# Attention's pair in another order on TensorE, VectorE and ScalarE

## The chip, the cores and the metric

One NeuronCore of a Trainium2 chip runs the whole program in one launch. The metric is the device time of one execution in microseconds, from three timed runs.

## The reference, cut to what matters

Four layers work on x, 32 batches of 128 tokens of 144 channels. The first three each hold an attention block and an MLP; the fourth rotates the tokens by a matrix exponential. Only attention is touched:

```python
B, L, C = (8, 128, 144); H = 16; D = C // H          # called with 32 batches
h = _modulate(_layernorm(x), shift_msa, scale_msa)
qkv = h @ W_qkv + b_qkv                              # 144 -> 432
scores = jnp.einsum('blhd,bmhd->bhlm', q * scale, k)
attn = jax.nn.softmax(scores, axis=-1)
o = jnp.einsum('bhlm,bmhd->blhd', attn, v).reshape(b, l, c)
x = x + gate_msa * (o @ W_proj + b_proj)
```

## The kernel before, in words

Each engine runs a list of its own, written out by hand, and waits on semaphores. Attention goes over 16 pairs of batches a layer (`for i in range(NP): pair(i)`); in `pair(i)` the even batch is e = 2i and the odd one o = 2i + 1. The steps of several pairs are interleaved: `at(lag)` tells whether pair i - lag exists, so a call with e - 4 is the even batch of two pairs ago, and one with i + 2 prepares tokens two pairs ahead.

The way of one batch, with the lines of the profile:

- VectorE normalises the tokens (`normalise`, L505 and L508, into xh). TensorE transposes both batches of a pair (`turn`, L1413 and L1414, into PSUM bank 5). ScalarE applies scale and shift (`h_modulate`, four instructions, L1072 and L1074, into hf and hs) and casts the high parts (`h_high`, L1086 and L1087). VectorE makes the low parts (`h_second`, which calls `low_parts`, L511 and L512). This splitting into high and low fp32r parts is the token rounding.
- TensorE multiplies by the QKV weights (`qkv_product`, four matmuls, L1399), into bank 4. ScalarE copies q and k (`qkv_high`, L1099) and V (L1100), and doubles the high parts (`qk_double`, L1107). VectorE writes the low parts of q and k (`qk_low`, L539).
- TensorE transposes q and k (`qk_turned`, four transpositions for each of j = 0 to 3, L1441; j = 0, 1 are the even batch, 2, 3 the odd one; bank 4, for j = 3 bank 5). ScalarE copies them (`qk_copy`, L1114, into Q and KK).
- `scores(b1, b2, a)` (L1456 and L1463) is 16 matmuls: the scores of b1 as rows, for the maximum, into PSA, and those of b2 transposed, for the exponential, into PSB. VectorE takes the row maximum (`row_max`, L544, two of a batch). TensorE transposes it (`max_turn`, L1491), and VectorE adds it into Q (`max_row`, L552). ScalarE takes the exponential of the second scores (`exps`, L1124, two of a batch).
- `pv` (L1480, 16 matmuls, two of a batch) writes bank 6; ScalarE copies it (`out_copy`, L1130); TensorE turns it back (`out_back`, L1501); VectorE divides (`inverse_sums`, L561, `normalise_out`, L566); TensorE transposes again (`out_turn`, L1506 and L1507); ScalarE copies (`oT_copy`, L1136 and L1137); TensorE projects (`project`, L1511 and L1512). VectorE multiplies by the gate (`gated_at`, L516) and adds to x, with new statistics (`update`, L521 and L524).

Waits that matter here: `pv(b, .., 1)` waits for the output copy of the batch before, since there is one bank for PV. `qkv_product(P, 1)` waits for the KK copy of j = 1, which is in the same bank. `scores(b1, b2, a)` waits for the maxima of b1 taken so far, for `max_row(b2)` and for the exponentials of the batch before. `h_modulate(P)` waits for `h_second(P - 1)`. SP loads a gate row for a batch once the update three batches before is done. GpSimd works on a QR factorisation, apart from all this.

The calls before the first pair are `pair(-2)` and `pair(-1)`; `passage` leads from the last pair into the MLP. In some pairs further work is queued: casts and splits of the MLP weights (pairs 2 to 6; in layer 1 these are four times as wide) and the steps of the deviations.

## Time and profile before

| | |
|---|---|
| three timed runs | 1269.46 us median, 1266.23 to 1276.68 |
| profiled execution | 1270.11 us, its span 1267.7 us |
| TensorE, matmuls | 1194.4 us busy, 94% of the span |
| VectorE | 910.0 us, 72% |
| ScalarE | 788.0 us, 62% |
| GpSimd | 749.6 us, 59% |
| chain of work that ended last | TensorE 82%, VectorE 13%, issue 4%, ScalarE 2% |

The share of busy time is an average over stages. Attention's pairs run from about 40 to 235 us (layer 0), 343 to 550 us (layer 1) and 915 to 1115 us (layer 2). Matmuls are pipelined: what a block costs TensorE is read from its start to the start of the next block.

### The profile page before, as it was taken

To read this page: it belongs to the slowest core of one execution; us is meant where nothing else is said; L and a number is where in the kernel's file an instruction comes from. 1 tells how busy PE (TensorE), PEld (TensorE's weight loads), DVE (VectorE), ACT (ScalarE), POOL (GpSimd) and SP (SyncE) were. 2 spreads that over 40 slices of the span, in tenths; PEclk is the share of its full clock that TensorE was granted. 3 is DMA by queue.
4 is the path that set the end of the run, shared out by engine and by line. 5 is a ranking of instruction groups with operands and counts; after the bars stand their busy time and mean duration, and the time that the engine had idled before them with its cause. 6 is when DMAs were issued, how large, how long until landed. Compare 5 with 4: busy or idle time off the path is not lost.

```text
span 1267.7 us, 35439 instructions
## 1 busy us (share of the span) xinstructions
PE 1194.4 (94%) x12778; PEld 949.3 (75%) x12778; DVE 910.0 (72%) x2496; ACT 788.0 (62%) x1809; POOL 749.6 (59%) x2230
## 2 busy tenths in 40 slices
PE   4899999899899999999999999999899999999997
PEld 2677777688676777778888888887777777777775
DVE  6799999766579999965575555554679999955432
ACT  3589898756479898963342333233379888874531
POOL 5656656666656656566676666667777777740000
PEclk9999999999979999999999999999969999989997
DMA  6321121242531121130210111120121111101130
GB/s 171 62 19 19 18 23 16 48 97 33 107 67 20 15 21 16 21 57 5 16 14 5 16 15 7 13 44 20 35 43 27 31 35 33 23 6 20 19 66 28
DMA packets 50319, 42.82 MB, mean 34 GB/s; under 512 B 8455, under 2 KB 45754, under 8 KB 49717
## 3 DMA queue, kind: packets, MB, share of 16 engines
q1 hardware_dynamic: 45884, 29.91, 10.9%
q0 software_dynamic: 3488, 8.52, 8.4%
q8 instruction: 104, 1.70, 0.6%
q10 hardware_dynamic: 780, 2.17, 0.5%
q14 instruction: 63, 0.52, 0.1%
HBM read 33.86 MB, written 3.03 MB: 29 GB/s over the span
## 4 chain that ended last, share of the span: by engine, by line
PE 82%; DVE 13%; issue 4%; ACT 2%; DMA 0%; SPq 0%; ACTq 0%; DVEq 0%
PE PS L1678 18%; PE PSA L1399 15%; PE PSA L1456 8%; PE PS L1480 8%; PE PS L1441 7%; PE PS L1399 6%; DVE BIG L544 3%; PE PSB L1651 2%; PE PS L1511 2%; PE PS L1501 2%; PE PS L1512 2%; PE PSB L1463 1%; PE PS L1506 1%; PE PS L1491 1%; DVE xh L508 1%
## 5 line engine op out<-in xcount | busy, mean ns | idle before, releaser
L1255 ACT ACTIVATE BIG<-PSA 128x512 f32<-128x512 f32 (+1 forms) x224 | 132.0, 593 | 264.1 <-PE PSA L1399 264.0
L1678 PE MATMUL PS<-w,BIG 128*128 128x144 f32 (+1 forms) x1920 | 254.7, 287 | 7.6 <-DVE BIG L818 4.1
L544 DVE TENSOR_REDUCE BIG<-PSA 128x8 f32<-128x1024 f32 x192 | 234.1, 1219 | 31.9 <-PE PSA L1456 29.9
L1678 PEld LDWEIGHTS PS<-w,BIG 128*128 128x128 f32 (+1 forms) x1920 | 245.1, 190 | 15.6 <-DVE BIG L818 4.9
L1124 ACT ACTIVATE BIG<-PSB 128x1024 f32<-128x1024 f32 x192 | 195.5, 1018 | 20.5 <-PE PSB L1463 20.3
L1456 PEld LDWEIGHTS PSA<-KK,Q 32*128 32x128 f32 x1536 | 109.9, 196 | 57.8 <-issue 41.0
L1456 PE MATMUL PSA<-KK,Q 32*128 32x128 f32 x1536 | 135.1, 294 | 14.9 <-DVE BIG L544 4.7
L1441 PE MATMUL PS<-K,qt 128*128 128x128 f32 x768 | 127.3, 293 | 10.4 <-DVE qt L539 4.8
L1463 PE MATMUL PSB<-Q,KK 32*128 32x128 f32 x1536 | 133.9, 293 | 0.0
L1480 PE MATMUL PS<-BIG,VA 128*32 128x128 f32 x3072 | 128.5, 287 | 1.1 <-DVE col L419 1.1
L1893 POOL MEMSET qprod<- 128x2 f32 x63 | 6.2, 99 | 203.0 <-DMA VB<-QA 203.0
L1875 POOL TENSOR_TENSOR qtree<-qtree 128x36 f32<-128x36 f32 (+3 forms) x384 | 104.3, 272 | 30.1
L1441 PEld LDWEIGHTS PS<-K,qt 128*128 128x128 f32 x768 | 91.3, 148 | 34.4 <-DVE qt L539 17.6
L1463 PEld LDWEIGHTS PSB<-Q,KK 32*128 32x128 f32 x1536 | 106.2, 195 | 1.2 <-DVE Q L552 0.4
L1399 PE MATMUL PSA<-hhi,Mhi 128*128 128x512 f32 (+1 forms) x224 | 99.9, 446 | 3.1 <-DVE h L512 2.1
L818 DVE SCALAR_TENSOR_TENSOR BIG<-PS,BIG 128x144 f32<-128x144 f32 x96 | 34.9, 367 | 94.6 <-PE PS L1678 94.0
L1880 POOL TENSOR_TENSOR qtree<-qtree 128x4 f32<-128x4 f32 (+3 forms) x384 | 83.7, 218 | 30.0
L1480 PEld LDWEIGHTS PS<-BIG,VA 128*32 128x32 f32 x3072 | 74.6, 112 | 30.2 <-issue 20.8
L1399 PE MATMUL PSA<-h,MW 128*128 128x512 f32 (+1 forms) x224 | 88.6, 395 | 0.0
L1399 PE MATMUL PSA<-hhi,Mlo 128*128 128x512 f32 (+1 forms) x224 | 88.5, 395 | 0.0
L1399 PE MATMUL PSA<-hlo,Mhi 128*128 128x512 f32 (+1 forms) x224 | 88.1, 393 | 0.0
L1099 ACT ACTIVATE qt<-PS 128x288 fp32r<-128x288 f32 x93 | 41.2, 443 | 56.5 <-PE PS L1399 56.5
(307 smaller groups left out, 2955.8 us busy)
## 6 DMA issues: line engine op xcount, KB each, us to landing
gate<-gates SPq DMA_DIRECT2D x96, 72.0 KB, 2.9
mgate<-gates SPq DMA_DIRECT2D x96, 72.0 KB, 2.7
VB<-skew POOLq DMA_DIRECT2D x16, 288.0 KB, 3.7
X<-in_x SPq DMA_DIRECT2D x4, 576.0 KB, 11.4
out<-X SPq DMA_DIRECT2D x8, 288.0 KB, 3.6
BIG<-in_skew_w SPq DMA_DIRECT2D x2, 1024.0 KB
w<-in_w SPq DMA_DIRECT2D x1, 1440.0 KB, 11.4
BIG<-in_wqkv SPq DMA_DIRECT2D x2, 584.0 KB
```

The costliest lines, as they stand in the source:

```text
L544: V.tensor_reduce(nmax.rearrange("p (s w) -> p s w", w=HP)[:, 2 * a:2 * a + 2, 3 * HD:3 * HD + G], PSA[:, :].rearrange("p (r g k) -> p r g ...
L1099: S.activation(qt[:, s, :, :, 0:HD], src, ACT.Copy).then_inc(qk_hi, 1)
L1124: S.activation(PT[:, u % 2, a, :], PSB[:, :], ACT.Exp, scale=float(HD) ** -0.5).then_inc(exp_done, 1)
L1255: S.activation(hm[0:rows, slot, :], PS[(par * FTOT[l] + j) % 2][0:rows, :], gelu).then_inc(gelu_done, 1)
L1399: last = mm(o, a, b, start=(k == 0), stop=(k == 3))
L1441: last = nc.tensor.transpose(turn_bank(pn, j)[:, g * 128:(g + 1) * 128], qt[:, s, j % 2, 4 * g:4 * g + 4, :].rearrange("p h w -> p (h w)") ...
L1456: one = mm(PS[r][:, g * 128:(g + 1) * 128], Q[rows, par, g, q0:q0 + 128], KK[rows, par, g, q0:q0 + 128], start=True, stop=True)
L1463: two = mm(PS[2 + r][:, g * 128:(g + 1) * 128], KK[rows, par, g, q0:q0 + 128], Q[rows, par, g, q0:q0 + 128], start=True, stop=True)
L1480: last = mm(PS[6][p0:p0 + HP, at:at + 128], VA[:, u, G * g + 2 * a + r, :], PT[:, u % 2, a, (G * r + g) * 128:(G * r + g + 1) * 128], star ...
L1678: last = mm(o, hm[0:rows, slot, s * 128:(s + 1) * 128], w2[0:rows, FT * e + k, :], start=(k == 0), stop=(k == FT - 1))
L1875: link(R.tensor_tensor(t[:, 0:n, :], a[:, :, 0:half], a[:, :, half:2 * half], ALU.add))
L1880: link(R.tensor_tensor(t[:, 0:n, :], a[:, :, 0:half], a[:, :, half:2 * half], ALU.add))
```

## The change

The same instructions run in another order, and two of them wait for something else.

- Token rounding: `h_high(i + 2)` follows `h_modulate(i + 2)` at once, in the same pair; `h_second(i + 2)` stands near the end of the same pair. Before, both were at the start of the next one. Only pair 0 of layers 1 and 2 still makes `h_high(1)` and `h_second(1)` itself.
- The output copy of an odd batch (`out_copy`) is made in the next pair, its update half a pair later than before.
- The even batch: `qk_low` waits for the copy of q and k alone, not for that of V. V's copy, now `v_copy`, waits until `qk_low` has read, and the transposition of q (`qk_turned` with j = 0) waits for V's copy.
- VectorE adds the even batch's maximum (`max_row`) ahead of `qk_low`.
- TensorE: PV of the even batch moves from the start of a pair to behind its first half's QKV product, both transpositions of the odd batch's k and q follow one another, the odd batch's QKV product stands behind the last `max_turn`, and `out_turn` of the even batch ends the pair.
- ScalarE: the odd batch's `qk_double` and the even batch's `oT_copy` are at the end of the pair.
- The prologue calls the steps of `pair(-2)` by name on VectorE, and `passage` is fitted to the new limits of the pair.

The diff, with 16 blanks of indentation taken off:

```diff
--- before.py
+++ after.py
@@ -531,9 +531,9 @@
     n0 = 256 * (P == NP + 1)
     low_parts(0 if P >= NP else P % 2, n0, n0 + 256)
-def qk_low(pn, s):
-    dve.wait_ge(v_ev, 2 * pn + s + 1)
+def qk_low(pn, s, before_v=False):
+    dve.wait_ge(qk_hi if before_v else v_ev, 2 * pn + s + 1)
     ps = qkv_bank(pn, s)[:, 0:2 * C].rearrange("p (k h w) -> p k h w", k=2, h=NH)
     for k, at in ((0, 2 * HD), (1, HD)):
         last = V.tensor_tensor(qt[:, s, k, :, at:at + HD], ps[:, k], qt[:, s, k, :, 0:HD].bitcast(F32), ALU.subtract)
@@ -571,7 +571,7 @@
 def update(b):
     added(n_gated(l, 0) + b, n_batch(l, 0) + b, b)
-def pair(i, dev=None, stats=None, late=None):
+def pair(i, dev=None, late=None):
     def at(lag):
         return 0 <= i - lag < NB // 2
@@ -584,10 +584,10 @@
     if at(0):
         row_max(e, 0)
     step(0)
-    if 0 <= i + 1 < NL:
-        h_second(i + 1)
-    if stats:
-        first_stats(stats)
+    if i == 0 and l:
+        h_second(1)
+    if 0 <= o - 6 < NB:
+        update(o - 6)
     if late:
         late(0)
     step(1)
@@ -603,13 +603,13 @@
         inverse_sums(o - 4, o % 2)
         normalise_out(o - 4, o % 2)
     step(4)
-    if at(-1):
-        qk_low(NP * l + i + 1, 0)
-    step(5)
     if at(0):
         max_row(e, e % 4)
     if late:
         late(2)
+    step(5)
+    if at(-1):
+        qk_low(NP * l + i + 1, 0, True)
     step(6)
     if 0 <= i + 2 < NL:
         normalise((e + 4) % NB, e % 4)
@@ -635,8 +635,8 @@
     step(12)
     if at(0):
         max_row(o, o % 4)
-    if 0 <= o - 4 < NB:
-        update(o - 4)
+    if 0 <= i + 2 < NL:
+        h_second(i + 2)
     if at(-1):
         qk_low(NP * l + i + 1, 1)
     if dev:
@@ -650,7 +650,7 @@
 def passage(rows, low, ones):
     b = NB - 4
-    h_second(NL - 1)
+    update(b - 1)
     gated_at(b, 0)
     update(b)
     inverse_sums(b + 1, 1)
@@ -975,10 +975,13 @@
     first_stats(0)
     columns(0, PS[1])
     deviations(0, 0, 0)
-    pair(-2)
+    normalise(0, 0)
+    normalise(1, 1)
     qkv_split(0)
     dve.wait_ge(h3_set, 1)
-    pair(-1, stats=1)
+    attentions[0][2](0)
+    first_stats(1)
+    pair(-1)
     V.memset(MW3[:, :].bitcast(F32), 0.0).then_inc(s_const, 1)
     first_stats(2)
     first_stats(3)
@@ -1086,7 +1089,7 @@
     S.activation(hhi[:, 0 if P >= NP else P % 2, n0:n0 + 256], hf[:, n0:n0 + 256], ACT.Copy)
     S.activation(hshi[:, n0:n0 + 256], hs[:, n0:n0 + 256], ACT.Copy).then_inc(hhi_ready, 1)
-def qkv_high(pn, s):
+def qkv_high(pn, s, with_v=True):
     n, ps = 2 * pn + s, qkv_bank(pn, s)
     act.wait_ge(qkv_ps, n + 1)
@@ -1097,6 +1100,13 @@
         act.wait_ge(va_zero, 1) if l < 2 else act.wait_ge(va_set, 2)
     src = ps[:, 0:2 * C].rearrange("p (k h w) -> p k h w", k=2, h=NH)
     S.activation(qt[:, s, :, :, 0:HD], src, ACT.Copy).then_inc(qk_hi, 1)
+    if with_v:
+        v_copy(pn, s)
+def v_copy(pn, s):
+    n, ps = 2 * pn + s, qkv_bank(pn, s)
+    wait(act, pv_done, n - 3)
     S.activation(V_heads(n % 4), ps[:, 2 * C:WC].rearrange("p (j h w) -> p j h w", j=2, h=8), ACT.Copy)\
         .then_inc(v_ev, 1)
@@ -1142,50 +1152,53 @@
         return 0 <= i - lag < NB // 2
     e, o, pn = 2 * i, 2 * i + 1, NP * l + i
-    last = 0 <= o - 2 < NB
-    if 0 <= i + 1 < NL:
-        h_high(i + 1)
-    if at(0):
+    if i == 0 and l:
+        h_high(1)
         qk_double(pn, 1)
     if rest:
         rest()
-    if at(2):
-        oT_copy(e - 4, e % 2)
-    if last:
+    if 0 <= o - 2 < NB:
         exps(o - 2, o % 2, 1)
     if at(0):
         qk_copy(pn, 2)
+        qk_copy(pn, 3)
+    if 0 <= o - 4 < NB:
+        out_copy(o - 4, o % 2)
+    if at(-1):
+        qkv_high(pn + 1, 0, False)
+    if 0 <= o - 2 < NB:
+        exps(o - 2, o % 2, 0)
+    if at(-1):
+        qk_double(pn + 1, 0)
+    if 0 <= o - 4 < NB:
+        oT_copy(o - 4, o % 2)
+    if at(-1):
+        act.wait_ge(qk_lo, 2 * (pn + 1) + 1)
+        v_copy(pn + 1, 0)
     if at(1):
         out_copy(e - 2, e % 2)
     if at(0):
-        qk_copy(pn, 3)
-    if at(-1):
-        qkv_high(pn + 1, 0)
-        qk_double(pn + 1, 0)
-    if last:
-        exps(o - 2, o % 2, 0)
-    if 0 <= o - 4 < NB:
-        oT_copy(o - 4, o % 2)
+        exps(e, e % 2, 1)
     if at(-1):
         qk_copy(pn + 1, 0)
-    if at(0):
-        exps(e, e % 2, 1)
+    if 0 <= i + 2 < NL:
+        h_modulate(i + 2)
+        h_high(i + 2)
     if at(-1):
         qk_copy(pn + 1, 1)
-    if 0 <= i + 2 < NL:
-        h_modulate(i + 2)
-    if last:
-        out_copy(o - 2, o % 2)
     if at(0):
         exps(e, e % 2, 0)
     if at(-1):
         qkv_high(pn + 1, 1)
+    if at(1):
+        oT_copy(e - 2, e % 2)
+    if at(-1):
+        qk_double(pn + 1, 1)
 def passage(gelus, modulate, cast):
     b = NB - 4
-    h_high(NL - 1)
-    oT_copy(b, 0)
+    out_copy(b + 1, 1)
     exps(b + 3, 1, 1)
     out_copy(b + 2, 0)
     exps(b + 3, 1, 0)
@@ -1433,6 +1446,8 @@
     pn, s = NP * l + P, j // 2
     pe.wait_ge(qk_lo, 2 * pn + s + 1)
     pe.wait_ge(qk_dup, 2 * pn + s + 1)
+    if j == 0:
+        pe.wait_ge(v_ev, 2 * pn + 1)
     if j == 1 or j == 2:
         pe.wait_ge(qk_rd, 4 * pn + j)
     elif j == 3:
@@ -1519,59 +1534,57 @@
     e, o = 2 * i, 2 * i + 1
     now = at(0)
     before = 0 <= o - 2 < NB
-    if at(1):
-        pv(e - 2, (e - 2) % 4, 1)
-    if at(2):
-        out_turn(e - 4, e % 2)
     if now:
         pe.wait_ge(qk_rd, 4 * (NP * l + i) + 2)
     scores(e if now else None, o - 2 if before else None, 0)
-    if at(1):
-        pv(e - 2, (e - 2) % 4, 0)
-    if now:
-        qk_turned(i, 2)
     if at(2):
         project(e - 4, e % 2)
     if now:
+        qk_turned(i, 2)
         qk_turned(i, 3)
     scores(e if now else None, o - 2 if before else None, 1)
     if at(-1):
         qkv_product(i + 1, 0)
     if 0 <= o - 4 < NB:
         out_back(o - 4, o % 2)
+    if at(1):
+        pv(e - 2, (e - 2) % 4, 1)
+    if now:
+        max_turn(e)
+    if at(1):
+        pv(e - 2, (e - 2) % 4, 0)
+    if 0 <= o - 4 < NB:
+        out_turn(o - 4, o % 2)
+    if now:
+        pe.wait_ge(qk_rd, 4 * (NP * l + i + 1))
+        scores(o, e, 0)
+    if at(-1):
+        qk_turned(i + 1, 0)
+    if 0 <= o - 4 < NB:
+        project(o - 4, o % 2)
+    if 0 <= i + 2 < NL:
+        turn(i + 2, i % 2)
     if before:
         pv(o - 2, (o - 2) % 4, 1)
     if now:
-        max_turn(e)
-    if 0 <= o - 4 < NB:
-        out_turn(o - 4, o % 2)
-    if at(-1):
-        qk_turned(i + 1, 0)
-    if now:
-        pe.wait_ge(qk_rd, 4 * (NP * l + i + 1))
-        scores(o, e, 0)
-    if 0 <= o - 4 < NB:
-        project(o - 4, o % 2)
-    if at(-1):
-        qk_turned(i + 1, 1)
-    if 0 <= i + 2 < NL:
-        turn(i + 2, i % 2)
-    if now:
         scores(o, e, 1)
-    if before:
-        pv(o - 2, (o - 2) % 4, 0)
     if at(1):
         out_back(e - 2, e % 2)
     if at(-1):
-        qkv_product(i + 1, 1)
+        qk_turned(i + 1, 1)
+    if before:
+        pv(o - 2, (o - 2) % 4, 0)
     if now:
         max_turn(o)
+    if at(-1):
+        qkv_product(i + 1, 1)
+    if at(1):
+        out_turn(e - 2, e % 2)
 def passage(first, turn_rows):
     b = NB - 4
     pv(b + 2, 2, 1)
-    out_turn(b, 0)
     scores(None, b + 3, 0)
     pv(b + 2, 2, 0)
     project(b, 0)
```

## Rows read from the trace of the kernel before

**Rows 1.** Windows by stage: PE, PEld, DVE, ACT, POOL busy, granted clock, DMA share, GB/s.

```profile
150.00:175.00 25.00, 24.65 (x372) 19.10 (x376) 23.73 (x56) 22.38 (x56) 15.92 (x46) 1.00 0.22 19
...
350.00:375.00 25.00, 24.16 (x278) 18.33 (x275) 17.78 (x46) 19.59 (x41) 14.37 (x44) 0.70 0.28 66
```

**Rows 2.** Timeline of TensorE over one pair: start, duration, line, tiles, idle before.

```profile
144.33 0.29 PE L1456 MATMUL PSA<-KK,Q 32*128 32x128 f32 x1
...
144.93 0.51 PE L1511 MATMUL PS<-wp,BIG 128*128 128x144 f32 x2
...
145.52 0.60 PE L1441 MATMUL PS<-K,qt 128*128 128x128 f32 x4
145.96 0.27 PE L1413 MATMUL PS<-K,xh 128*128 128x128 f32 x1
...
146.49 0.32 PE L1456 MATMUL PSA<-KK,Q 32*128 32x128 f32 x1
...
147.09 0.65 PE L1480 MATMUL PS<-BIG,VA 128*32 128x128 f32 x16
...
147.86 0.44 PE L1399 MATMUL PS<-Ahi,hhi 128*128 128x432 f32 x1
...
148.73 0.27 PE L1491 MATMUL PS<-K,BIG 128*128 128x128 f32 x1
148.93 0.64 PE L1480 MATMUL PS<-BIG,VA 128*32 128x128 f32 x16
149.51 0.33 PE L1506 MATMUL PS<-K,BIG 128*128 128x128 f32 x1
...
149.98 0.29 PE L1456 MATMUL PSA<-KK,Q 32*128 32x128 f32 x1
...
153.27 0.46 PE L1399 MATMUL PS<-Ahi,hhi 128*128 128x432 f32 x1
...
154.16 0.38 PE L1501 MATMUL PS<-K,BIG 128*128 128x128 f32 x2
154.47 0.65 PE L1480 MATMUL PS<-BIG,VA 128*32 128x128 f32 x16
...
155.66 0.66 PE L1441 MATMUL PS<-K,qt 128*128 128x128 f32 x4
156.45 0.29 PE L1456 MATMUL PSA<-KK,Q 32*128 32x128 f32 x1
```

**Rows 3.** Timeline of VectorE in the same pair.

```profile
153.38 1.23 DVE L544 TENSOR_REDUCE BIG<-PSA 128x8 f32<-128x1024 f32 x1 [0.38 <-PE PSA L1456]
...
155.09 0.51 DVE L539 TENSOR_TENSOR qt<-PS,qt 128x144 fp32r<-128x144 f32 x2
155.52 0.68 DVE L552 TENSOR_TENSOR Q<-Q,PS 128x512 fp32r<-128x512 f32 x1
```

**Rows 4.** Timeline of ScalarE in the same pair and the next.

```profile
154.36 0.44 ACT L1099 ACTIVATE qt<-PS 128x288 fp32r<-128x288 f32 x1 [0.98 <-PE PS L1399]
154.68 0.29 ACT L1100 ACTIVATE VA<-PS 128x144 f32<-128x144 f32 x1
154.85 0.45 ACT L1107 ACTIVATE qt<-qt 128x288 fp32r<-128x288 f32 x1
...
156.09 0.29 ACT L1136 ACTIVATE BIG<-PS 128x128 f32<-128x128 f32 x1
156.25 0.25 ACT L1137 ACTIVATE BIG<-PS 17x128 f32<-17x128 f32 x1
...
158.28 0.60 ACT L1114 ACTIVATE KK<-PS 128x512 fp32r<-128x512 f32 x1
158.77 0.45 ACT L1072 ACTIVATE hf<-PS,col 128x128 f32<-128x128 f32 x1
...
160.14 0.38 ACT L1130 ACTIVATE BIG<-PS 128x256 f32<-128x256 f32 x1
```

**Rows 5.** Timeline of VectorE in the first pair of layer 1.

```profile
347.56 0.52 DVE L539 TENSOR_TENSOR qt<-PS,qt 128x144 fp32r<-128x144 f32 x2 [1.16 <-ACT VA L1100]
```

## The prediction

> **What bounds the kernel now.** I read four views, in this order. The busy shares and slices of the page say where to look: 48 attention pairs, 16 in each of three layers, take well over half of the span, and the edit touches only them. The windows by stage then show that in a steady stretch of 25 us TensorE is busy for 24.65, VectorE for 23.73 and ScalarE for 22.38 [rows 1]: three engines almost full, so no single total sets the time, the order does. The timeline of TensorE over one pair gives the period: the scores that open with line 1456 at 144.33 come again at 156.45, so 12.12 us [rows 2]. TensorE's starts follow one another nearly without a hole, but each kind of block has its own start-to-start cost, and these costs, with the few places that are longer than usual, are what I use.
>
> The places that are longer: the transpositions of q and k at 155.66 take 0.79 to the next scores, where the same block took 0.44 before another transposition and the four token transpositions 0.53 before scores [rows 2]. Two VectorE hand-offs lie there. The low parts (line 539) start at 155.09 and end at 155.60, and the transpositions start 0.06 later; the row maximum's addition (line 552) ends at 155.52 + 0.68 = 156.20, and the scores start 0.25 later [rows 2, 3]. So about 0.26 us here, and I estimate 0.2 ahead of 155.66, are TensorE waiting for VectorE: 0.45 to 0.5 us of each pair. VectorE itself stood idle 0.38 for the scores [rows 3]. That is the whole stake: were every wait gone, TensorE's present order would need about 11.65 us.
>
> **The new TensorE order at its own costs.** No matmul is added or dropped. I add up the 23 blocks in the new order with the old start-to-start costs, all from [rows 2]: scores 0.60 (144.33 to 144.93; 146.49 to 147.09); projection right behind scores 0.59; q/k transpositions 0.44, or 0.53 if scores or PV follow; QKV product behind scores 0.89, elsewhere 0.87; PV 0.58; back-transposition ahead of PV 0.31; max transposition ahead of PV 0.20; output transposition behind PV, ahead of scores, 0.47. Four places have no row and are estimates from these: q/k transpositions behind scores 0.54 (0.44 and the 0.10 by which blocks behind scores are longer), a projection elsewhere 0.49, back-transposition behind scores 0.32, max transposition ahead of QKV 0.11; output transposition ahead of scores but behind QKV 0.31.
> First part, to the end of the first out_turn: 0.60+0.59+0.44+0.53+0.60+0.89+0.31+0.58+0.20+0.58+0.47 = 5.79. Rest: 0.60+0.54+0.49+0.53+0.58+0.60+0.32+0.53+0.58+0.11+0.87+0.31 = 6.06. Sum 11.85 us. This is 0.2 more than the old order's 11.65, because scores now are followed by full-array blocks four times (before: twice) and PV is entered from full-array blocks four times. The floor therefore is only 0.27 us a pair under today's period.
> The rows show that price as 0.09 to 0.10 at the changes between scores, PV and full-array blocks. The Trainium skill (TensorEngine Tiling (Array Packing), Key Properties) says that changing the tiling mode drains TensorE; by that rule alone the new order, with 15 changes of mode a pair against 14, is slightly dearer, and speaks against the change. The sum goes by the rows.
>
> **VectorE.** The low parts of the even batch leave the chain that feeds the transposed maximum: they no longer wait for V (a wait of 1.16 at a layer's start [rows 5]), and they stand behind the maximum's addition. The chain from the second even scores to the next scores is then 0.71 (scores to the maximum) + 1.22 + about 0.3 + 0.93 (line 552 to scores, 155.52 to 156.45), some 3.2 us, under TensorE's 3.63 of blocks in between: the stall of 0.26 goes. The stall ahead of 155.66 goes too. Token rounding (h_second) moves from the start of the next pair to the end of this one; its inputs then need to be there sooner (below). The update of odd batches moves half a pair later; the gate loads on SP wait for it, but their row is next used more than a pair later, so nothing. Its work is cover for the first row maximum, so 0. The same VectorE work per pair remains, and at 23.73 of 25 us [rows 1] it fits a period of 12.1.
>
> **ScalarE, where new waits arise.** Let s be the start of a pair's first scores.
> (1) The odd QKV product now stands last but one, so it starts at s - 1.18 (0.87 + 0.31). A QKV product reaches ScalarE after 1.09 (153.27 to 154.36), the q/k copy costs 0.32 (154.36 to 154.68) and V 0.17 (to 154.85) [rows 2, 4]. oT_copy of the even batch is queued behind them and starts at s + 0.40; its two instructions end 0.41 later (156.09 to 156.25, and 0.25) [rows 4], at s + 0.81. The projection, wanted at s + 0.60, starts at s + 0.87: a wait of 0.27. Behind oT_copy is qk_double, ready in time. The same product feeds the odd low parts, which then stand just ahead of row_max on VectorE and delay it to about s + 1.0; its maximum is ready for the next scores near s + 2.4, the moment when TensorE gets there after the 0.27.
> (2) V of the even batch now waits for the low parts and is behind oT_copy of the odd batch; the q/k transpositions wait for it. out_turn to oT_copy 0.47, oT_copy 0.32, V 0.29 and 0.06 make 1.14, against TensorE's 0.47 + 0.60: 0.07, and up to 0.1 for starting cold. I take 0.1.
> (3) h_high now follows h_modulate at once, ahead of the KK copy, which the odd QKV product waits for (its PSUM bank). From the token transpositions: 0.64 to ScalarE (three of 0.11, 0.27 and 0.04), four modulations 1.37 (158.77 to 160.14), 0.11 until the last is written, two casts 0.61 (estimated; the double of 288 columns at 154.85 lasts 0.45), KK 0.60 to its end (158.28) [rows 4], 0.06: 3.39. TensorE gets there after 0.53+0.58+0.60+0.32+0.53+0.58+0.11 = 3.25. A wait of 0.14 to 0.2, taken as 0.15.
> What is late next is ScalarE, no longer VectorE: 0.27 + 0.10 + 0.15 = 0.52, so 11.85 + 0.52 = 12.37 us, 0.25 more than 12.12. Bounds of the three: none at all (if copies are issued ahead and the engine restarts at once), and 0.95 together if the 0.25 seen between line 552's end and the scores [rows 2, 3] is exposed at (1) and (3) as well, as a weight load that can't run ahead. So a period of 11.85 to 12.8.
>
> **How many pairs, and the edges.** Of 48 pairs the first two of each layer differ, and four of layer 1 carry extra weight casts and splits and are set by VectorE; I leave those four unchanged. 38 x 0.25 = 9.5 us longer. At each layer's first pair the maximum's addition no longer stands behind low parts that waited 1.16 for V [rows 5]; two of those starts give back about 0.8 each, the first layer 0.4: -2. The passage to the MLP gets its token rounding earlier and has one output copy and one update more: 0, with 1 us either way. The layer-0 prologue keeps its instructions: 0. Total +7.5. The profiled execution took 1270.11 (span 1267.7), 0.65 above the median of the three runs, 1269.46; on the median +7.5 gives 1277.
>
> **Rivals.** (a) The waits trade evenly: ScalarE's three come to 0.3, not 0.52, and the time stays, about 1269. For it: ScalarE has more slack than the other two [rows 1]. Against: its slack is not where the chains are. (b) The order works and none of the three waits is seen: 38 x -0.27 - 2 gives 1257. For it: both VectorE stalls really go; against: (1) is arithmetic on latencies that are all in the rows. (c) The granted clock: in the stretch 350 to 375 it is 0.70 on average [rows 1], a part at the lower level behind the idle start of the layer. If the closer first pair lets it rise sooner, 2 to 3 us at each of two layers come back: 1272. (d) Slower: the copies on ScalarE expose the weight load too, and (1) and (3) grow to about 0.5 and 0.3. Period 12.8, 38 x 0.68 - 2 = +24: 1293. It decides once qk/V copy, oT_copy and the projection chain exceed the one scores block that hides them, which they do already by 0.27.
>
> **Chances.** Forecast 0.42, (a) 0.13, (b) 0.10, (c) 0.07, (d) 0.28. Most of the range from (b) to (d) is needed for 8 in 10: 1260 to 1293. Within 1% (about what a measurement of this kernel tells from no change) is 1256.8 to 1282.2: the forecast, (a) and (c) with small tails give 0.57; slower by more than 1% is (d) and a tail, 0.33; faster 0.10.
>
> **What would show it.** After: period from scores to scores about 12.4; projection of the even batch 0.85 to 0.9 behind the scores' start, released by oT_copy; q/k transpositions released by V's copy; the odd QKV product released by KK; line 552 no longer a releaser of scores. The forecast is wrong if the period is under 12.1, which would mean that ScalarE's chain starts earlier than TensorE's order lets me place it, or if blocks in their new neighbourhoods do not cost what they did.

## The result, and the profile after

The changed kernel took 1296.08 us (median of 4 runs, 1294.45 to 1306.02) against 1267.85 (4 runs) on the same chip: ratio 1.0235, 95% interval 1.0152 to 1.0319. It is slower by about 28 us. The forecast was 1277 with a range of 1260 to 1293: the sign was right, the size was not.

The page of the changed kernel: its span, the busy times and the chain that ended last.

```profile
span 1294.1 us, 35483 instructions
...
PE 1208.5 (93%) x12778; PEld 960.6 (74%) x12778; DVE 906.2 (70%) x2496; ACT 797.9 (62%) x1809; POOL 745.4 (58%) x2230
...
PE 80%; DVE 11%; issue 4%; ACT 4%; DMA 0%; SPq 0%; ACTq 0%; DVEq 0%
```

ScalarE's share of the chain went from 2% to 4%, VectorE's fell from 13% to 11%. The window that answers to the first of [rows 1] shows all three engines less busy than before, so no engine became the bound; they wait for each other more. The last three columns of such a line are the granted clock of TensorE as a share of full speed, the DMA share and GB/s.

```profile
150.00:175.00 25.00, 24.24 (x356) 18.66 (x356) 22.77 (x53) 22.13 (x54) 15.67 (x46) 1.00 0.26 20
```

One quiet pair of layer 0 on TensorE, with one row for each block that matters (start, duration, line; the bracket is the idle time and its releaser). The scores at 153.38 open the pair, as the one at 144.33 does in [rows 2].

```profile
151.79 0.33 PE L1506 MATMUL PS<-K,BIG 128*128 128x128 f32 x1
152.21 0.43 PE L1412 MATMUL PS<-Ahi,hhi 128*128 128x432 f32 x1
...
153.07 0.27 PE L1521 MATMUL PS<-K,BIG 128*128 128x128 f32 x1
...
153.38 0.32 PE L1471 MATMUL PSA<-KK,Q 32*128 32x128 f32 x1
...
154.22 0.51 PE L1526 MATMUL PS<-wp,BIG 128*128 128x144 f32 x2 [0.18 <-ACT BIG L1147]
...
154.82 1.04 PE L1456 MATMUL PS<-K,qt 128*128 128x128 f32 x8
155.78 0.32 PE L1471 MATMUL PSA<-KK,Q 32*128 32x128 f32 x1
...
159.47 0.29 PE L1471 MATMUL PSA<-KK,Q 32*128 32x128 f32 x1
...
160.22 0.63 PE L1456 MATMUL PS<-K,qt 128*128 128x128 f32 x4
```

The three forecast waits are there. The projection (1526) starts 0.84 behind the scores instead of 0.60: 0.24. The even transpositions (1456) start 0.75 behind the scores at 159.47 instead of 0.60: 0.15. From the maximum's transposition (151.79) to the odd QKV product (152.21) it is 0.42 instead of 0.11: 0.31. Together 0.70. The rows of ScalarE name what released them.

```profile
151.18 0.40 ACT L1090 ACTIVATE hshi<-hs 51x256 fp32r<-51x256 f32 x1
151.49 0.57 ACT L1124 ACTIVATE KK<-PS 128x512 fp32r<-128x512 f32 x1
...
153.59 0.29 ACT L1110 ACTIVATE VA<-PS 128x144 f32<-128x144 f32 x1
153.75 0.29 ACT L1146 ACTIVATE BIG<-PS 128x128 f32<-128x128 f32 x1
153.91 0.26 ACT L1147 ACTIVATE BIG<-PS 17x128 f32<-17x128 f32 x1
...
159.80 0.28 ACT L1110 ACTIVATE VA<-PS 128x144 f32<-128x144 f32 x1
```

KK's copy (151.49) stands behind the second cast of token rounding and ends at 152.06, 0.15 ahead of the QKV product. The copy for the projection stands behind V (153.59). The even V copy ends at 160.08, 0.14 ahead of the transpositions.

The wait views agree for the projection. Over 63 to 229 us, which is layer 0 without its edges, this row heads the waits of TensorE's matmuls (weight loads apart) in the changed kernel (total us, times, longest):

```profile
PE PS L1526 <- ACT BIG L1147: 2.3, 13, 0.2
```

**Where the 26.4 us of span went.** I read the starts of line 552 of all even batches, pair by pair, in both traces. The differences, after less before:

| part | us |
|---|---|
| 21 pairs without casts or splits (12.48 against 12.12 in most, nearly equal where the deviations run) | +5.8 |
| 15 pairs, 2 to 6 of each layer, with casts and splits (most at 12.80 against 12.2 in layers 0 and 2, at 13.71 against 12.93 in layer 1) | +8.9 |
| pairs 0 and 1 | -0.8 |
| from pair 14's line 552 to the last one of each layer | +3.7 |
| outside the pairs: to the first pair -1.4, the two stretches from layer to layer +4.4 and +4.2, the end +1.5 | +8.8 |

So most quiet pairs lost 0.36, but the 21 together 5.8, which is 0.27 each, since those where the deviations run lost little. More than half of the loss lies where the prediction had 0 or little: pairs with extra work, and the ends of layers.

A part of it is TensorE's clock: over the whole program the changed kernel's profile shows 82.8 us at a granted 0.50, that of before 69.1. The times of two rows hang on where those stretches fall: in the last pair of layer 0 the odd addition comes 8.60 behind the even one, at half clock, and 5.60 in layers 1 and 2 (before 7.11 in layer 2, at half clock, and 5.72 and 5.29), so that +3.7 would be near 2.5 without; and in the kernel before the second interval of layer 2 is 14.82, partly at half clock, where layers 0 and 1 have 12.17 and 12.02, which by itself gives the -0.8 of pairs 0 and 1 its sign.

### The profile page after: what moved, and what is told of

It reads as the page before. It is cut to its first block, busy times and chain, and to the rows that moved or that the text cites. A ratio compares the mean times of both kernels' runs of the same rounds, so it can differ in the third digit from the quotient of the medians.

```text
span 1294.1 us, 35483 instructions
## 1 busy us (share of the span) xinstructions
PE 1208.5 (93%) x12778; PEld 960.6 (74%) x12778; DVE 906.2 (70%) x2496; ACT 797.9 (62%) x1809; POOL 745.4 (58%) x2230
## 4 chain that ended last, share of the span: by engine, by line
PE 80%; DVE 11%; issue 4%; ACT 4%; DMA 0%; SPq 0%; ACTq 0%; DVEq 0%
PE PS L1691 18%; PE PSA L1412 14%; PE PS L1495 8%; PE PS L1412 7%; PE PSA L1471 6%; PE PS L1456 6%; DVE BIG L544 3%; PE PSB L1664 2%; PE PS L1526 2%; PE PS L1516 2%; PE PS L1506 2%; PE PS L1527 1%; PE PSB L1478 1%; PE PS L1426 1%; DVE qt L539 1%
## 5 line engine op out<-in xcount | busy, mean ns | idle before, releaser
L1456 PE MATMUL PS<-K,qt 128*128 128x128 f32 x768 | 116.5, 288 | 7.3 <-ACT VA L1110 2.4
L1888 POOL TENSOR_TENSOR qtree<-qtree 128x36 f32<-128x36 f32 (+3 forms) x384 | 101.1, 263 | 30.1
L1893 POOL TENSOR_TENSOR qtree<-qtree 128x4 f32<-128x4 f32 (+3 forms) x384 | 81.1, 211 | 30.0
```

Source lines behind the costliest of these rows:

```text
L1456: last = nc.tensor.transpose(turn_bank(pn, j)[:, g * 128:(g + 1) * 128], qt[:, s, j % 2, 4 * g:4 * g + 4, :].rearrange("p h w -> p (h w)") ...
L1888: link(R.tensor_tensor(t[:, 0:n, :], a[:, :, 0:half], a[:, :, half:2 * half], ALU.add))
L1893: link(R.tensor_tensor(t[:, 0:n, :], a[:, :, 0:half], a[:, :, half:2 * half], ALU.add))
```

## The experiments

Each is an edit of one of the two kernels; quiet pairs are compared by the same line-552 starts. The edits are shown shortened to the calls that move. Medians of the kernel before on the same chips were 1268.1, 1269.5, 1266.9, 1268.0 and 1267.8 for the five groups of runs.

### What in the quiet pair costs 0.36

**Thinned work.** Both kernels, inner pairs alone: casts of token rounding 8 of 256 columns wide, exponentials 128 of 1024, row maxima over 16 of 128 keys.

```diff
-S.activation(hhi[..., n0:n0 + 256], hf[:, n0:n0 + 256], ACT.Copy)
+S.activation(hhi[..., n0:n0 + 8], hf[:, n0:n0 + 8], ACT.Copy)
```

> The kernel before, with ScalarE and VectorE made light inside the pairs (part of the computation is left out: the casts of the high parts on 8 of 256 columns, the exponentials on 128 of 1024 columns, the row maximum over 16 of 128 keys), so that TensorE's block order alone sets the period. My sum of block costs gives 11.6 to 11.7 us for a quiet pair. If copies still bind, 11.8.

> The changed kernel with the same parts of the work left out. By my sum of block costs in the new order, 11.85 us, 0.2 above the kernel before thinned alike. The rival, that the new period of 12.48 is TensorE's own cost of the new order, gives 12.3 to 12.5 here, and 0.35 more than the kernel before thinned alike.

> The changed kernel with only the high-part casts (h_high) on 8 of 256 columns in pairs' inner part (the rest of the tokens' high parts is left out), which takes about 0.4 us out of ScalarE's stretch between the token transpositions and the next projection and changes no order. If that stretch is one queue that closes the cycle (transposition of tokens, ScalarE, projection, TensorE, transposition), the quiet period falls by the 0.4 to about 12.1. If TensorE's order or VectorE sets it, it stays at 12.48.

Before, thinned: 1260.79 us, quiet period 12.13, so unchanged. After, thinned: 1274.12, quiet 12.33. After with the casts alone thinned: 1288.97, quiet 12.32 to 12.34. Each is a single execution, so the period counts here and not the total. The first is a miss for my theory. TensorE and VectorE of the thinned kernel before show why:

```profile
142.31 0.27 PE L1509 MATMUL PS<-K,BIG 128*17 128x128 f32 x1
142.57 0.66 PE L1443 MATMUL PS<-K,qt 128*128 128x128 f32 x4
143.37 0.29 PE L1458 MATMUL PSA<-KK,Q 32*128 32x128 f32 x1
```

```profile
141.49 0.26 DVE L561 RECIPROCAL BIG<-PS 128x16 f32<-128x16 f32 x1 [0.91 <-PE PS L1503]
141.78 0.31 DVE L566 TENSOR_TENSOR BIG<-PS,BIG 128x144 f32<-128x144 f32 x1
142.01 0.51 DVE L539 TENSOR_TENSOR qt<-PS,qt 128x144 fp32r<-128x144 f32 x2
142.44 0.68 DVE L552 TENSOR_TENSOR Q<-Q,PS 128x512 fp32r<-128x512 f32 x1
```

VectorE is idle for 0.91 now, and from the transpositions to the scores it is 0.80, as good as the 0.79 of [rows 2]. It is a chain of fixed steps from TensorE's own back-transposition through divisions, low parts and the maximum's addition to the scores. VectorE's load had nothing to do with it: in a window of 25 us it is busy for 16.25 here and for 23.73 in [rows 1]. In the changed kernel the same thinning gives 0.15, and the casts alone give all of it; they stand ahead of KK's copy. From the maximum's transposition to the odd QKV product it is 0.28 there, for 0.42 with full casts and 0.11 in the forecast: half of this wait stays without the casts. Row maxima and exponentials, together the largest work of VectorE and ScalarE, are worth nothing in a quiet pair of either kernel.

**Single swaps on ScalarE.** Three edits of the changed kernel.

```diff
 h_modulate(i + 2)
+qk_copy(pn + 1, 1)        # kk_first: KK copy ahead of the casts
 h_high(i + 2)
-qk_copy(pn + 1, 1)
```

```diff
-qkv_high(pn + 1, 1)       # tail_v: odd V copy last,
+qkv_high(pn + 1, 1, False)  # low parts wait for q and k alone
 oT_copy(e - 2, e % 2)
 qk_double(pn + 1, 1)
+act.wait_ge(qk_lo, 2 * (pn + 1) + 2)
+v_copy(pn + 1, 1)
```

```diff
+qk_turned(i, 2)           # proj_later, TensorE
 project(e - 4, e % 2)
-qk_turned(i, 2)
 qk_turned(i, 3)
...
+qk_double(pn + 1, 1)      # ScalarE
 oT_copy(e - 2, e % 2)
-qk_double(pn + 1, 1)
```

> The changed kernel, with the KK copy of the next even batch ahead of h_high on ScalarE. My prediction's account of separate waits: the odd QKV product, which starts 0.42 us behind the max transposition instead of 0.11, starts 0.18 sooner, and the quiet pairs take 12.3 us: 5 to 8 us faster. The rival: the end of the pair is one ScalarE queue (h_high, KK copy, exponential, q/k copy), so that what is taken from one wait comes back at the exponential that the next scores wait for: 12.4 to 12.55, no change.

> The changed kernel, with the odd batch treated as the even one: VectorE's low parts wait for the copy of q and k alone, ScalarE copies oT of the even batch right behind that copy, and V last. ScalarE theory: the projection starts 0.16 us sooner behind the pair's first scores (now 0.84), the row maximum 0.2 sooner, and the quiet pairs take 12.30 to 12.35 us instead of 12.48; in all 5 to 8 us faster, 1288 to 1291. The rival, that the longer period is what TensorE's block order costs by itself: no change of the period (12.45 to 12.5).

> The changed kernel with the odd batch's first transposition ahead of the even batch's projection on TensorE, and on ScalarE the odd doubling ahead of the copy for the projection, so that the projection has 0.5 us more and the transposition finds its parts ready. Theory A (the projection's wait of 0.24 us is a loss on TensorE's chain): quiet period 12.22 to 12.30, 1287 to 1289. Theory B (the pair is a cycle through TensorE, ScalarE and VectorE, and the copies of the odd k and q, 0.2 to 0.6 us later now, or the row maximum, take the wait's place): 12.45 to 12.55, 1295 to 1299.

KK first: 1301.56 us, ratio 1.0233, quiet 12.51. Odd V last: 1297.12, ratio 1.0237, quiet 12.55. Projection later: 1300.79, ratio 1.0268, quiet 12.70. None helps. With KK first, the casts stand ahead of the exponential and the odd q/k copy instead, in the same queue, and cost as much there: a pair's first scores now wait 0.27 for that exponential. The last one makes it worse than either theory had it. Its TensorE and VectorE rows:

```profile
154.95 0.66 PE L1455 MATMUL PS<-K,qt 128*128 128x128 f32 x4 [0.44 <-DVE qt L539]
```

```profile
154.38 0.52 DVE L539 TENSOR_TENSOR qt<-PS,qt 128x144 fp32r<-128x144 f32 x2 [0.34 <-ACT VA L1110]
```

The odd transposition, put in the projection's place, waits 0.44 for the odd low parts, which wait for the odd V copy. So the projection had covered it. Two things follow the odd QKV product at the pair's end, the copy for the projection, queued behind the product's own copies, and the transposition of its k. Both have one block of scores as cover, and in this run the wait taken from one fell on the other.

**Token rounding.** Alone on the kernel before, its ScalarE half alone, and undone in the changed kernel. The edits move the calls of `h_high` and `h_second` and little else (one wait of the prologue moves with them). In the kernel before, `h_high` then stands behind both KK copies and the odd output copy, and not right behind `h_modulate` as in the change.

> The kernel before with one part of the change alone: token rounding a pair sooner on ScalarE (the casts to high parts right behind the modulation, behind both KK copies, ahead of the second exponential of the even batch) and on VectorE (the low parts near the pair's end). TensorE's order, the waits of V and the output copies are those of before. Theory A (the loss is in TensorE's new order and in the fixed hand-offs it exposes, plus 0.15 us of the casts in ScalarE's end-of-pair queue): here the casts stand ahead of the odd output copy, the even exponential and the QKV copies, of which the output copy feeds the PV at the pair's start, so a little is lost: quiet period 12.15 to 12.30, time 1270 to 1276. Theory B (token rounding alone carries most of the loss): period 12.35 or more, 1282 or more. Theory C (it gains, since VectorE's low parts no longer stand behind the first row maximum): period 12.0, 1264.

> The kernel before with ScalarE's half of the sooner token rounding alone: the casts to high parts right behind modulation and odd output copy, ahead of the even batch's second exponential; VectorE makes the low parts at the start of the next pair as before. Rounding sooner as a whole gave a quiet period of 12.46 against 12.12. Theory A (the loss is VectorE's: 0.72 us of low parts in front of the odd batch's q/k low parts, which the transpositions wait for): quiet period 12.12 to 12.20, 1267 to 1272. Theory B (the loss is ScalarE's: casts of 0.62 us push the exponential and the q/k copy): 12.40 or more, 1282 or more.

> The changed kernel with token rounding undone alone: the casts to high parts and the low parts are again at the start of the next pair; TensorE's new order, the V copy and the output copies stay. Theory A (h_high ahead of the KK copy costs 0.15 us a pair, the rest is order): quiet period 12.30 to 12.36 as with the thinned casts, provided the casts at the start of the pair cover nobody; 48 x 0.15 less, so 1288 to 1291. Theory B (rounding sooner is what the new order needs, since ScalarE's start of the pair now has the odd exponential and two copies in a row): the period rises to 12.6 or more, 1300.

Alone: 1287.45 us, ratio 1.0179, quiet 12.46. ScalarE's half alone: 1270.83, ratio 1.0040, quiet 12.22. Undone in the changed kernel: 1320.47, ratio 1.0438, quiet 12.70. In the kernel before, rounding sooner costs 0.34 a pair, 0.10 by ScalarE's casts, which leaves 0.24 for VectorE's low parts. Here are VectorE and TensorE of the kernel before with rounding sooner:

```profile
157.32 0.41 DVE L511 TENSOR_TENSOR hlo<-hf,hhi 128x256 fp32r<-128x256 f32 x1
157.64 0.47 DVE L512 SCALAR_TENSOR_TENSOR h<-hshi,K,hs 51x256 fp32r<-51x256 f32 x1
158.04 0.51 DVE L539 TENSOR_TENSOR qt<-PS,qt 128x144 fp32r<-128x144 f32 x2
```

```profile
157.76 0.64 PE L1482 MATMUL PS<-BIG,VA 128*32 128x128 f32 x16
158.60 0.66 PE L1443 MATMUL PS<-K,qt 128*128 128x128 f32 x4 [0.20 <-DVE qt L539]
```

The token low parts (0.72) stand ahead of q's and k's, and the transpositions start 0.84 behind PV and not 0.58. In the new order the same step helps: undone, a quiet pair takes 0.22 more; with the casts at the start of the pair (156.27 below), the odd exponential comes later, and TensorE, which now reaches the second scores sooner, waits for it. ScalarE of the changed kernel with rounding undone:

```profile
156.27 0.40 ACT L1088 ACTIVATE hshi<-hs 51x256 fp32r<-51x256 f32 x1
156.58 1.00 ACT L1132 ACTIVATE BIG<-PSB 128x1024 f32<-128x1024 f32 x1
```

And TensorE's second scores there, which wait for that exponential:

```profile
157.72 0.29 PE L1470 MATMUL PSA<-KK,Q 32*128 32x128 f32 x1 [0.31 <-ACT BIG L1132]
```

**V's copy.** The whole V part alone on the kernel before (`qk_low(.., True)`, `v_copy` behind the odd `oT_copy`, the wait of j = 0), and undone in the changed kernel.

> The kernel before with V's part alone: the even batch's low parts of q and k wait for the copy of q and k and not for that of V, V is copied behind the odd batch's projection copy once the low parts have been read, and the transposition of q waits for V's copy. Nothing else is moved. The low parts in the kernel before start right behind the divisions on VectorE and not at V's copy, so no gain is expected from the earlier start. Theory A (V's copy sits in idle or full ScalarE time and is ready before the transposition): 12.12, 1267 to 1270. Theory B (the transposition gets V's copy as a new last wait, as in the changed kernel, where it costs 0.15): 12.2 to 12.3, 1273 to 1277.

> The changed kernel with V's part undone alone: V is copied right behind q and k, ahead of the exponential and the projection copy, and the even batch's low parts wait for V. Theory A (in the changed kernel V's late copy makes the even transpositions wait 0.15 us; undone, the low parts have slack behind the maximum's addition, so the wait goes to its 0.02 or 0): quiet period 12.33 to 12.40, 1289 to 1293. Theory B (V ahead pushes exponential, doubling and projection copy by 0.17, and the copy for the projection ends as late as V did): 12.48 to 12.55, 1296 to 1299.

Alone: 1315.86 us, ratio 1.0346, quiet 13.05. Undone: 1335.08, ratio 1.0547, quiet 13.36. Both far outside what any theory expected. In the kernel before, V's copy is now behind an exponential and the copy for the projection, and the transposition stands close behind the product. TensorE with V's part alone:

```profile
154.95 0.63 PE L1453 MATMUL PS<-K,qt 128*128 128x128 f32 x4 [1.16 <-ACT VA L1107]
```

In the changed kernel without it, the reason is a buffer. V has four buffers, so the copy of batch n waits for PV of batch n - 4, and the new order has moved just this PV (of `e - 2`) behind the QKV product. TensorE and ScalarE of the changed kernel with V back:

```profile
152.00 0.64 PE L1492 MATMUL PS<-BIG,VA 128*32 128x128 f32 x16
```

```profile
152.71 0.30 ACT L1110 ACTIVATE VA<-PS 128x144 f32<-128x144 f32 x1 [1.21 <-PE PS L1492]
```

ScalarE, in order, stands for 1.21 us with an exponential queued behind. So V's late copy is no improvement in itself (alone, 0.93 more a pair): it is what makes the moved PV bearable.

### What the pairs with casts and splits cost

```diff
+mlp_cast(l, i - 3)        # cast_mid, ScalarE: pairs 3 to 6,
 qkv_high(pn + 1, 0, False)  # not behind pairs 2 to 5
...
 update(e - 4)             # split_mid and before_split, VectorE
+mlp_split(l, i - 4)       # ahead of this maximum, pairs 4 to 7,
 row_max(o, 1)             # not behind pairs 3 to 6
```

> The changed kernel, with the casts of the MLP weights on ScalarE issued in the middle of pairs 3 to 6, where it idles 0.66 us ahead of the even q/k copy, instead of between pairs, behind qk_double. ScalarE theory: the end of a pair is ScalarE's critical stretch, and the casts lengthen it; the pairs with casts fall from 12.80 to 12.5 to 12.6 in layers 0 and 2 and from 13.71 to 13.0 to 13.3 in layer 1; in all 4 to 6 us faster, about 1291. The rival, that VectorE's splits of the same weights set these pairs: no change.

> The changed kernel, with VectorE's splits of the MLP weights issued ahead of the odd batch's second row maximum, where VectorE idles 0.5 us, instead of between pairs, where the low parts and the first row maximum follow. Moving the casts on ScalarE left the pairs at 12.80. If VectorE's queue at the seam of two pairs is what the splits lengthen, the pairs with splits fall from 12.80 to 12.5 to 12.6 in layers 0 and 2 and from 13.71 to 13.2 to 13.4 in layer 1, together 3 to 4 us. If not, no change.

> The kernel before with one move on VectorE: the splits of the MLP weights stand ahead of the second row maximum of the odd batch in pairs 4 to 7 and not behind pairs 3 to 6. Theory A (splits at the pair's end stand in front of the next pair's first row maximum, on the chain that bounds the pair; in the middle they partly fill idle time): layer 1's four pairs of 12.93 fall to about 12.5, 1.5 to 2 us less in all, 1266 to 1268. Theory B (VectorE is simply full in these pairs, place doesn't matter): no change, 1268 to 1269.

Casts moved in the changed kernel: 1296.25 us, ratio 1.0225; pairs with a split stay at 12.80, only the one without fell. Splits moved in the changed kernel: 1291.11, ratio 1.0217 (interval 1.0129 to 1.0304, which holds the changed kernel's 1.0235); split pairs of layer 2 fall from 12.80 to 12.67, in layer 1 from 13.71 to between 13.14 and 13.98. The 15 pairs lose 7.3 us then and not 8.9, so the place of the splits is worth 1.6. The profile is 7.1 us shorter in all, but 4.9 of that lie outside the pairs and 2.6 in the last ones, where nothing was moved and the clock fell at other times. Splits moved in the kernel before: 1270.95, ratio 1.0025, layer 1 at 12.92 to 13.09, no gain. The place of the splits in the changed kernel, on VectorE:

```profile
410.34 0.52 DVE L539 TENSOR_TENSOR qt<-PS,qt 128x144 fp32r<-128x144 f32 x2 [0.33 <-ACT VA L1110]
410.78 0.75 DVE L460 TENSOR_TENSOR Mlo<-BIG,Mhi 128x577 fp32r<-128x577 f32 x1
411.44 0.82 DVE L461 SCALAR_TENSOR_TENSOR MW<-MW,K,BIG 51x577 fp32r<-51x577 f32 x1
412.19 1.21 DVE L544 TENSOR_REDUCE BIG<-PSA 128x8 f32<-128x1024 f32 x1
```

The low parts wait 0.33 for V, and only then come 1.41 us of splits ahead of the first row maximum. In the kernel before the same splits cost 0.8 of a pair, here 1.2. With the casts of token rounding thinned, two of layer 1's split pairs stand at 13.55, with maxima and exponentials thinned too at 12.62: here, other than in quiet pairs, the amount of this work counts. Whether it is VectorE's maxima or ScalarE's exponentials, no run separates.

### What the end of a layer costs

```diff
+if i == NP - 1:           # passage_copy, ScalarE, last pair
+    out_copy(o - 2, o % 2)
 oT_copy(e - 2, e % 2)
...
-out_copy(b + 1, 1)        # at the head of passage
```

```diff
+if i == NP - 1: fill(3)   # fill_after: the last pair repeats its QKV product thrice
```

> The changed kernel, with TensorE repeating the first QKV product three times (12 matmuls, results never read) in the last pair of each layer, where no next pair is to be prepared; output unchanged. The clock theory: the 8.8 us that the changed kernel loses outside the pairs come from TensorE's granted clock, which is 0.50 from 234 to 254 us and again at 564 to 572 us, behind the thinly filled last pair. If so, the clock stays at 1.00 there, the stretch from the last line-552 addition of layer 0 to the first one of layer 1 falls from 117.9 to 113 to 115 us, and the whole gets 4 to 8 us faster, 1288 to 1292. The rival, that those 8.8 us are instructions moved out of the pairs into the passage: the added matmuls only cost their own time, 2 to 3 us per layer at most, and the kernel gets 0 to 6 us slower.

> The changed kernel with one move on ScalarE in the last pair of each layer: the odd batch's output copy is made there, ahead of the even batch's copy for the projection, and no longer in the passage. Theory A (part of the 9 us that the change costs outside the pairs' starts is this copy, which the PV of the next batch waits 0.78 us for at the head of the passage): the wait goes, 0.5 to 0.8 us in each of three layers, 1294 in all, and where TensorE's clock had fallen in this stretch it may fall later. Theory B (the passage's cost is the clock's alone): the wait goes, the passage is no shorter beyond 0.3 us, 1296.

> The changed kernel with both moves: the odd output copy inside the last pair ahead of the projection's copy, and the MLP splits ahead of the second odd row maximum. Alone they gave 1289 (first) and 1291 (second) where the changed kernel has 1296. If the two are separate losses they add up: 1284 to 1287, ratio to before 1.013 to 1.017. If the first one's gain was only the place where the clock happened to fall, the run gives 1290 to 1292 and its granted clock in the passages is again at the lower level.

> pass_split with the edit of proj_later. Theory A: 1285 less 9, so 1276 to 1279, still above the kernel before at 1268. Theory B: 1284 to 1288, as pass_split alone.

Filling TensorE: 1300.6 us, ratio 1.0253, last pairs 14.83 and not 12.9, so slower, as the rival had it. Its clock part came true in layer 0, where the clock did not fall and the stretch to the next layer took 114.8 and not 117.9; at the end of layer 1 the clock fell all the same. The copy in the last pair: 1288.95 (1284.96 to 1291.71), ratio 1.0189 (interval 1.0119 to 1.0259, which overlaps the changed kernel's). With the splits moved as well: 1284.89, ratio 1.0147 (1.0098 to 1.0195), inside the 1284 to 1287 expected if the two are separate losses. With the later projection on top: 1292.28, ratio 1.0214; quiet pairs 12.71, its loss is carried over. None beats the kernel before.

In the changed kernel the odd output copy (1140) of the last pair stands behind the even copy for the projection (1147) and the PV of the next batch waits for it. ScalarE, then TensorE:

```profile
243.35 0.25 ACT L1147 ACTIVATE BIG<-PS 17x128 f32<-17x128 f32 x1
243.50 0.36 ACT L1140 ACTIVATE BIG<-PS 128x256 f32<-128x256 f32 x1
```

```profile
242.72 0.42 PE L1522 MATMUL PS<-K,BIG 128*17 128x128 f32 x1
...
243.92 1.08 PE L1495 MATMUL PS<-BIG,VA 128*32 128x128 f32 x16 [0.78 <-ACT BIG L1140]
```

With the copy moved, ScalarE and TensorE at the same place:

```profile
238.97 0.36 ACT L1140 ACTIVATE BIG<-PS 128x256 f32<-128x256 f32 x1
239.35 0.28 ACT L1146 ACTIVATE BIG<-PS 128x128 f32<-128x128 f32 x1
```

```profile
239.04 0.27 PE L1523 MATMUL PS<-K,BIG 128*17 128x128 f32 x1
239.39 0.64 PE L1496 MATMUL PS<-BIG,VA 128*32 128x128 f32 x16
```

The durations differ as well: 1.08 for a PV and 0.64. The windows over this stretch say why (the third column from the end is the granted clock), first the changed kernel, then the one with the copy moved:

```profile
232.00:236.00 4.00, 3.57 (x61) 2.15 (x61) 3.67 (x10) 1.60 (x4) 3.24 (x12) 0.79 0.11 23
236.00:240.00 4.00, 4.00 (x48) 3.10 (x44) 2.06 (x4) 2.56 (x6) 2.88 (x7) 0.50 0.02 5
240.00:244.00 4.00, 3.22 (x37) 1.79 (x37) 3.01 (x6) 2.40 (x7) 1.10 (x4) 0.50 0.40 36
```

```profile
236.00:240.00 4.00, 3.37 (x71) 1.99 (x63) 3.68 (x10) 3.73 (x10) 3.33 (x9) 1.00 0.10 25
240.00:244.00 4.00, 4.00 (x52) 3.47 (x49) 2.77 (x11) 2.75 (x4) 0.66 (x4) 1.00 0.57 36
```

From 234 to 255 us the changed kernel's TensorE ran at a granted 0.50, which is 1.2 GHz, the other at 2.4. I counted such falls from ten us before to twenty us behind the start of a layer's last line 552. In the eight profiles of the changed pair's order with the copy in the passage (the changed kernel, KK first, odd V last, casts moved, splits moved, filled, projection later, casts thinned) there are 15 in 24 layers; in the three with the copy in the last pair, 0 in 9. Three more profiles have the copy in the passage: the changed kernel thinned (0 in 3), with V's part undone (0 in 3) and with rounding undone (3 in 3), so 18 in 33 in all. The kernel before has 1 in 3, and with its five edits 6 in 18. So the move takes away the wait, and its profiles show no fall at a layer's end; but the copy in the passage alone does not bring one. Nor are falls gone elsewhere: with the copy moved there is one at 421 us, in a pair of layer 1 that then takes 15.96, and the mean granted clock of the timed runs is 0.967 against 0.963 in the changed kernel and 0.972 to 0.976 in the five groups of the kernel before.

The stretches from layer to layer tell what each is worth. In the eight profiles, the seven stretches behind a layer end without a fall are 0.7 to 1.8 us longer than in the kernel before; the nine with one are 2.5 to 5.7 longer. With the copy moved, the six stretches are between 0.7 shorter and 0.7 longer. So the wait for the copy costs about 1 us a layer, and most of the +4.4 and +4.2 is the lower clock.

How the copy could lead to the falls is not shown: it is waited for 0.78 us at the end of every layer of the changed kernel, and the fall begins 0.7 and 1.2 us behind that wait in layers 1 and 2, but in layer 0 near 234, nine us before it. The Trainium skill (TensorE: Matmul & The Clock Gate, Part 1: The HAM clock gate) says that the number of matmuls at the lower clock behind a start varies from run to run of the same kernel. No run here shows that for one kernel, since each has one profile; but layer 0 has no fall in three of the eight, and so the counts and not one profile are the evidence.

## Why the prediction was wrong

Its reasoning held within a quiet pair, and its books outside it did not. It forecast 7.5 us more, and the profiles show 26.4. The 18.9 that are missing: passage and end of the program 10.2, pairs with casts and splits 6.1, last pairs 2.2, quiet pairs 0.5 (the edges came to 0.1 less than forecast).

**TensorE's own cost, 11.85.** Right. The period 12.48 less the waits of 0.70 is 11.78, and the thinned kernel gives 11.77. Reading the cost of a block start to start, by what follows it, works for an order that has never run, to 0.08 us. Two single costs were off by about as much and cancelled: q/k transpositions behind scores 0.46 and not 0.54, the maximum's transposition ahead of PV 0.26 and not 0.20. The Trainium skill's rule (TensorEngine Tiling (Array Packing), Key Properties) that a change of tiling mode drains TensorE asked for no more than the rows already had, and no run here shows the drain apart from them.

**The VectorE stalls go.** Right for TensorE: the scores at 159.47 have no wait on line 552. But I had "three engines almost full" as the frame, and the thinned kernel before shows that VectorE's fullness was not it: the stall was a chain of fixed steps.

**The three waits, 0.52.** Right in kind, place and releaser. (1) the projection 0.24 for 0.27. (2) the transposition behind V 0.15 for 0.10. (3) the odd QKV product behind KK 0.31 for 0.15; the thinned casts give back half of it, and from KK's end to the product it is 0.15 where the sum had 0.06. Term (3) was mis-sized, the rest is small: period 12.48 for 12.37. On the 21 quiet pairs that made 5.8 for 5.25, because the pairs with deviations lost little, which is luck.

**"38 x 0.25", and four pairs "unchanged".** This is one of the two steps that failed. 15 pairs carry casts or splits and lost 8.9 us, 0.59 each on average and 0.8 in most of layer 1. I had 2.75: eleven of them at 0.25 like quiet pairs, and four of layer 1 at 0, since I reasoned that those are set by VectorE and stay. The change puts token low parts, and low parts that wait for V, into the same place at the pair's end, so the splits are added behind a wait. Moving them gives back 1.6 of the 8.9, and 13.71 falls to 12.62 only where maxima and exponentials are thinned; what sets the rest stays open. The last pairs were also in the 38, at 1.5 for all, and lost 3.7, near 2.5 without the clock.

**The passage, "0, with 1 us either way".** This is the other failed step, and the larger one: +4.4, +4.2 and +1.5 from the ends of the three layers on. I counted the output copy at the head of `passage` as one more instruction and did not ask who waits for it. PV does, for 0.78 in each layer. Where the clock stayed up, that made 0.7 to 1.8 us a layer, already more than the 1 us that I allowed for all of it; the larger part is the granted clock, which I had looked at only for the starts of layers and which fell to 0.50 at each layer's end. With the copy moved, the median is 1288.95, some 7 us less, and the profile's span is 11.6 us shorter, by 12.3 outside the pairs. Why the clock falls there stays open.

**The edges, -2.** The sum is nearly right, by luck: pairs 0 and 1 gave 0.8 and the start 1.4, but the 0.8 is one interval of the kernel before at the lower clock (14.82). Apart from it, these pairs became longer, by 1.8. The gain itself is there, but ahead of the first mark: from the start of the first even batch's second maximum to its addition it is 1.96 for 2.81 in layer 1 and 2.11 for 2.48 in layer 2, where I had 0.8 each.

**The rivals.** (d), slower at 1293, came nearest in time, by another road: its price of 0.68 a pair from an exposed weight load is not what the rows show. (a) and (b) need smaller waits and are out. (c) was right that the clock moves the time, but it did so the other way and elsewhere: it fell at the ends of layers. At the start of layer 2 the changed kernel does have 17 us at the lower clock where the kernel before has 24; at that of layer 1 both have 20.

**What I did not ask.** Which parts of the change are its cost? I weighed rounding and V as refinements. Alone on the kernel before they cost 20 and 48 us, and undone in the changed kernel 24 and 39. They are conditions of the new TensorE order and losses without it. What remains as the cost of that order itself, net of them, is in my reading the pair's end: the odd QKV product last but one, whose copies and low parts have one block of scores as cover. TensorE's order alone, the later output copy and the sooner addition of the even maximum were not run by themselves.

## What to carry to other kernels

When an engine that is nearly full waits for another that is nearly full, thin the other one before blaming its load: here row maxima of an eighth of the keys changed nothing in a quiet pair. When a block is moved, list the buffers that it frees and who queues for them; V's copy waited 1.21 us for a PV that had moved. Cost the pairs that carry extra work and the last one as carefully as the quiet ones, since they were 12.6 of 26.4 us, and the passage 8.8.

## What the runs showed that I had not expected

One ScalarE copy of 0.36 us at the end of each layer, moved ahead of the two instructions of the projection's copy, went with some 7 us off the median, and its three profiles show no fall of the granted clock at nine layer ends, where the profiles with the copy in the passage have 18 in 33. A fall there is worth more than the wait itself: stretches with one were 2.5 to 5.7 us longer than before, those without 0.7 to 1.8. Repeating the QKV product three times there to keep TensorE busy did not always prevent the fall (0.50 from about 566 to 576 us in layer 1). What makes the clock fall at these places stays open.
